# Two chained deformable-convolution blocks on one core: half-strip tap products on quarters of the array, and a new split between half-strips and gathered tiles

## The reference, cut to what matters

```python
x = x + relu(bn(deform_conv(_gn(x), offsets=conv3x3(_gn(x)))))        # L0, offsets below one pixel
v = _gn(x)
om1 = conv2d(v, w_om1, b_om1)                                         # 18 offsets + 9 masks per pixel
out = gelu(bn(modulated_deform_conv(v, offset1, sigmoid(m1), w_dcn1)))   # C1
om2 = conv2d(out, w_om2, b_om2)
out = modulated_deform_conv(out, offset2, sigmoid(m2), w_dcn2)        # C2
x = x + gelu(bn(out) + v)

# modulated_deform_conv: for each pixel and each of 9 taps, a bilinear sample at a data-dependent place
py = ys - PAD + ki + off[:, :, 0]; px = xs - PAD + kj + off[:, :, 1]
samp = bilinear_gather(x, py, px) * mask
out = einsum('bckhw,ock->bohw', samp, weight)
```

## Time and profile before

| | |
|---|---|
| median of the runs shown | 6692.59 us (6688.65 to 6696.53) |
| profiled execution, span | 6690.3 us |
| PE busy | 6000.0 us, 90% |
| DVE busy | 4534.0 us, 68% |
| ACT busy | 2208.6 us, 33% |
| POOL busy | 4608.7 us, 69% |
| indirect DMAs on POOL (L895) | 4752 = 132 tiles of 36, mean 967 ns |
| granted TensorE clock, mean | 0.928 |

### The profile page before, as it was taken

One profiled execution on the slowest core, in us unless ns is written; L12 is line 12 of the kernel. 1 busy time (PEld: TensorE's weight loads), 2 busy tenths in 40 slices (PEclk: granted clock), 3 DMA queues, 4 the chain that ended last, 5 costly groups with the idle time before them and its releaser, 6 DMA issues. The chain is left out here.

```text
span 6690.3 us, 124828 instructions
## 1 busy us (share of the span) xinstructions
PE 6000.0 (90%) x48293; PEld 4792.9 (72%) x48293; DVE 4534.0 (68%) x8624; ACT 2208.6 (33%) x3376; POOL 4608.7 (69%) x4765
## 2 busy tenths in 40 slices
PE   6997998987988988998987998899989989998996
PEld 6886777766777767777765666677767777776775
DVE  6886776856777856777754555477667767676675
ACT  1222222232222222222322222244434444443442
POOL 0005777766777767777777777777777777777776
PEclk9998999988999988999987898899989999998998
DMA  5334344435343433444422332333333334333333
GB/s 148 99 99 116 100 112 114 113 88 141 100 112 104 119 82 108 109 111 107 110 79 75 82 78 73 98 87 84 84 94 95 91 80 103 91 88 86 87 84 77
DMA packets 505472, 653.42 MB, mean 98 GB/s; under 512 B 116137, under 2 KB 412121, under 8 KB 496985
## 3 DMA queue, kind: packets, MB, share of 16 engines
q0 software_dynamic: 152064, 311.73, 18.8%
q1 hardware_dynamic: 352856, 333.94, 17.7%
HBM read 599.16 MB, written 46.15 MB: 96 GB/s over the span
## 5 line engine op out<-in xcount | busy, mean ns | idle before, releaser
L895 POOL DMA_INDIRECT G<-table,IDX x4752 | 4594.6, 967 | 2036.7 <-issue 1932.9
L2282 DVE TENSOR_TENSOR ARENA<-ARENA,OUT 128x864 f32<-128x864 f32 x936 | 937.5, 1048 | 142.7 <-PE RED L1123 94.7
L1517 ACT ACTIVATE SAMP<-RED 96x384 f32<-96x384 f32 x688 | 335.2, 487 | 1889.8 <-PE RED L1335 824.9
L1123 PE MATMUL RED<-IDENT,ARENA 128*96 128x128 f32 x7344 | 876.1, 279 | 73.0 <-DVE ARENA L2282 73.0
L2085 DVE TENSOR_TENSOR G<-G,WPS 128x1152 f32<-128x1152 f32 x528 | 711.1, 1347 | 309.3 <-DMA G<-table,IDX 308.0
L1123 PEld LDWEIGHTS RED<-IDENT,ARENA 128*96 128x96 f32 x7344 | 816.5, 129 | 117.4 <-issue 114.3
L1316 PE MATMUL BTP<-PAD,ARENA 80*128 x2304 | 748.5, 448 | 56.8 <-DVE ARENA L2078 29.9
L1072 PE MATMUL OFF<-PAD,ARENA 128*54 128x128 f32 (+1 forms) x10944 | 748.5, 295 | 12.7 <-ACT PAD L1417 6.8
L1072 PEld LDWEIGHTS OFF<-PAD,ARENA 128*54 128x54 f32 (+1 forms) x10944 | 666.9, 134 | 112.9 <-issue 97.5
L1196 PE MATMUL BTP<-X 80*128 80x480 f32 x1248 | 648.7, 638 | 105.8 <-ACT X L1461 57.0
L1512 ACT ACTIVATE SAMP<-RED 96x384 f32<-96x384 f32 x528 | 257.3, 487 | 1450.4 <-PE RED L1138 733.7
(11 more groups left out here) (216 smaller groups left out, 7777.7 us busy)
## 6 DMA issues: line engine op xcount, KB each, us to landing
ARENA<-wtab SPq DMA_DIRECT2D x416, 400.0 KB
G<-table,IDX POOLq DMA_INDIRECT x4752
ARENA<-xo SPq DMA_DIRECT2D x96, 720.0 KB
X<-xo SPq DMA_DIRECT2D x80, 360.0 KB, 3.8
table<-TB SPq DMA_DIRECT2D x64, 384.0 KB, 2.5
X<-x SPq DMA_DIRECT2D x3, 3200.0 KB, 18.2
out<-X SPq DMA_DIRECT2D x20, 320.0 KB
wtab<-TB SPq DMA_DIRECT2D x16, 384.0 KB, 3.1
```

Source lines behind the costliest of these rows:

```text
L895: pool.indirect_dma_start(G[:, b, k, :], None, tables[seg.table], bass.IndirectOffsetOnAxis(ap=IDX[:, q, b * TAPS + k:b * TAPS + k + 1], a ...
L1123: last = nc.tensor.matmul(RED[b % 2][0:TPG * C, gr * 128:(gr + 1) * 128], PROD[gr][:, sft, :], IDENT[:, :], start=(sft == 0), stop=(sft == ...
L1517: nc.scalar.activation(SAMP[:, x], RED[x][0:TPG * C, 0:GROUPS * 128].rearrange("p (g n) -> p g n", g=GROUPS), ACT.Copy).then_inc(z.samp_re ...
L2282: nc.vector.tensor_tensor(out=PROD[gr].rearrange("p (dy dx) (j c) -> p j dy dx c", dy=3, j=TPG), in0=win.rearrange("p j dy (dx c) -> p j d ...
```

## The change

Half-strips: the 80 columns are cut in two overlapping sides of 64 columns that lie on partitions 0 to 63 and 64 to 127 (`XW`, `XSTEP`). For one tap there are now four matmuls of 64x64 by 64x480, one for each side and image: side picks the array's rows and the PSUM bank, the image picks the array's columns. So one bank holds both images of one side, and both banks are filled by each tap; the next tap waits until both are read. The 18 products on DVE and the six groups of 15 transposing matmuls stay as many. The tents are made in two pieces, taps 0 to 4 and taps 5 to 8, on 128 partitions in place of 80. Samples of a half-strip go to `SAMP1` in three copies in place of two.

Split: pairs 0 to 2 use rows 32 to 64 for half-strips (16 of them) and have 17 gathered tiles. Kind x is not used any more: the mix is 26 d and 14 f, "ddf" * 8 + "df" and "ddf" * 4 + "df". Tail and pair 3 keep their steps. In a step with a successor of kind f, the first piece of the next tents stands on ACT ahead of the tile's last sample and the half-strip's last sample.

```diff
-MIXED_C = "xdxdfd" + "xdxfd" * 3, "xdxdfd" + "xdxdf"
+MIXED_C = "ddf" * 8 + "df", "ddf" * 4 + "df"
-C1_ROWS = {0: (32, 48), 1: (32, 48), 2: (32, 48), 3: (32, 64)}
+C1_ROWS = {0: (32, 64), 1: (32, 64), 2: (32, 64), 3: (32, 64)}
+XW, XSTEP = 64, W - 64
+TX_TAPS = (0, 5), (5, TAPS)
...
-                def taps_half(half, im, gr):
+                def taps_half(half, k):
...
-                        if c >= len(TAPS1[p]):
-                            pe.wait_ge(weighted1, c + 1 - len(TAPS1[p]))
-                        row = strip_row(seg, t // 2) + t % 2 * 2 + k // 3 - 1 - BELOW1 - r0
-                        nc.tensor.matmul(TAPS1[p][c % len(TAPS1[p])][:, 0:TAPW1], TX1[p][im][:, k, :],
-                                         XT1[p][:, im, row:row + WY1, :].rearrange("p w c -> p (w c)"),
-                                         start=True, stop=True).then_inc(taps1, 1)
+                    if h or k:
+                        pe.wait_ge(weighted1, 18 * h + 2 * k)
+                    row = strip_row(seg, t // 2) + t % 2 * 2 + k // 3 - 1 - BELOW1 - r0
+                    for side in range(2):
+                        ps_ = slice(XW * side, XW * side + XW)
+                        for im in range(2):
+                            last = nc.tensor.matmul(BTP[side][64 * im:64 * im + 64, 0:TAPW1], TX1[p][ps_, k, im, :],
+                                                    XT1[p][ps_, im, row:row + WY1, :].rearrange("p w c -> p (w c)"),
+                                                    start=True, stop=True)
+                        last.then_inc(taps1, 1)
...
+                def weight_half(half, k):
+                    for side in range(2):
+                        at = 2 * gr + side
+                        if j == 0:
+                            dve.wait_ge(prod_used, half.wg + GROUPS + max(0, at - 1))
+                        dve.wait_ge(taps1, 18 * half.i + 2 * k + side + 1)
...
                     if half.prep:
                         on.offsets(*half.prep)
-                    tile_sample(2)
+                    if step.ahead:
+                        on.tents1(*step.ahead, 0)
                     tile_sample(3)
-                    half_sample(1)
+                    half_sample(2)
                     if half.prep:
                         on.mask(*half.prep)
```

More of the change, by code:

```diff
@@ L1233, in consume_both @@
                         pe.wait_ge(e, column_evacs(half.seg.p, side))
-                    tiles = [(b, 0, step.po, b // 2) for b in range(UNITS)]
-                    halves = [(im, 1, half.po, 0) for im in range(2)]
-                    on.taps_half(half, 0, 0)
+                    on.taps_half(half, 0)
                     if step.prep:
                         on.convolve(*step.prep)
-                    on.taps_half(half, 0, 1)
-                    on.reduce_half(half, 0, 0)
+                    on.taps_half(half, 1)
@@ L1251, in consume_both @@
-                    on.reduce_half(half, 1, 0)
-                    on.project_units(step, [tiles[1], halves[0]], 5)
+                    on.reduce_half(half, 0, 0)
+                    on.taps_half(half, 3)
+                    on.reduce_half(half, 1, 0)
+                    on.project_tile(step, 0)
+                    on.taps_half(half, 4)
+                    on.turn_unit(step, 1)
+                    on.taps_half(half, 5)
+                    on.project_tile(step, 1)
+                    on.reduce_half(half, 0, 1)
@@ L1788, in constants1 @@
                         nc.vector.memset(to.iota[:, w:w + 1], float(w))
-                    nc.vector.memset(to.column[:, 128:256], 0.0)
-                    nc.vector.tensor_copy(to.below_row, BASE_Y[:, 0:1])
-                    for c in range(TC):
-                        nc.vector.tensor_scalar(to.steps[:, c:SCOLS:TC], BASE_X[96:98, 0:SCOLS // TC * TAPS:TAPS], float(c), None, ALU.add)
-                    last = nc.vector.scalar_tensor_tensor(out=to.negp, in0=BASE_Y[0:W, 0:1], scalar=-float(TC), in1=BASE_X[0:W, 0:1],
+                    nc.vector.memset(to.column[:, 128:182], 0.0)
@@ new lines, in constants1 @@
+                    half_cols, half_taps = SCOLS // 2, SCOLS // 2 // TC * TAPS
+                    for side in range(2):
+                        for c in range(TC):
+                            nc.vector.tensor_scalar(to.steps[:, side * half_cols + c:(side + 1) * half_cols:TC],
+                                                    BASE_X[96:98, side * half_taps:(side + 1) * half_taps:TAPS], float(c - XSTEP * side), None, ALU.add)
+                    last = nc.vector.tensor_scalar(to.below_row, BASE_Y[:, 0:1], float(XW // TC), -float(XW // TC), ALU.is_ge, ALU.mult)
@@ L1847, in prepare_half_strips @@
                     after(0)
+                    places = turned(seg, t)[:, :, :, 1:2 * TAPS:2]
+                    most, least = (m.rearrange("p (tt side k) -> p tt side k", tt=2, side=2) for m in (lent_.smax, lent_.sneg))
+                    nc.vector.scalar_tensor_tensor(out=most[:, :, 0], in0=places[:, :, 0], scalar=float(WY1 - XW), in1=most[:, :, 0],
+                                                   op0=ALU.add, op1=ALU.max)
+                    nc.vector.scalar_tensor_tensor(out=least[:, :, 1], in0=places[:, :, 1], scalar=-1.0, in1=least[:, :, 1],
+                                                   op0=ALU.mult, op1=ALU.max)
                     nc.vector.tensor_scalar(FLAT[:, :].rearrange("p (tt im k) -> p tt im k", tt=2, im=2), turned(seg, t)[:, :, :, 0:2 * TAPS:2],
```

255 lines of the change are left out of this document (144 added, 111 removed).

## The result

The changed kernel takes 7,035.97 us (median; 7,035.38 to 7,036.55) against 6,692.59: a ratio of 1.0517 with a 95% interval of 1.0492 to 1.0543. It is slower. The prediction was 7,073 with a range of 6,815 to 7,315 and a chance of 0.83 for slower.

A forecast was written before the change was run, and what follows sets the result against it. POOL was taken to run near its pace with PE right behind, so steps were priced on PE: 6690.3 us plus 359 for mixes and 21 for tails, 7,070, with 2.3 over the profiled span 7,073 us; range 6,815 to 7,315.

The forecast's parts named there:

- The mixes: Pairs 0 to 2: 26 d and 14 f steps make 949 us each, 359 us more in all than before.
- the tails: Ends of pairs 0 to 2: 7 us more per pair, 21 us more together.
- POOL's 540 us are a gain: Pairs 0 to 2: 12 gathered tiles fewer per pair shorten the kernel; chance 0.07, most of it within 2%.
- PE stands right behind POOL: Kernel before: POOL runs close to its pace throughout, with PE busy 715.8 of 786.4 us in pair 1's mix.
- A dense step of 16.6 us: Each d step in the mixes of pairs 0 to 2 stays at 16.6 us.
- Four quarters at once: Taps on PE: a tap's four products run together, 0.9 us per tap, 8.1 us for nine.
- two at a time: Rival for the taps: 1.7 us per tap, f steps of 38.5 and 47 us, 7,315 us in all; chance 0.12.
- An even f step: Mixes: 27.1 us of PE work plus 5.7 us of waits, 32.8 us against 35.6 before.
- An odd f step: Mixes: adds convolution and an end stall on DVE; next d starts at 39.7 us, 41.1 with the slower clock.
- The tents ahead of the samples: Last f of a mix: first tents wait on offsets through DRAM and delay the last samples, 7 us more per pair.
- The first f behind the norm: Tails of pairs 0 to 2: the one f with a gain there saves 2.8 us.
- Pair 3 and C2: 69 tiles at POOL's pace, about 46 us each; the two stages give and cost nothing.

The follow-up runs named there:

- The quarters alone: Changed kernel with the earlier split of tiles and half-strips put back, four quarter matmuls per tap kept: 6,650.07 us, ratio 0.9937 against the kernel before.

## Why the prediction was right, point by point

**The method held.** I priced steps on PE, not tiles on POOL. The forecast was +380 us and +343 was measured. The mixes came 7 us above their forecast of +359, the tails 50 us below theirs, and the head and the stages behind added 6 that had been put at nothing. Close as the total is, it is no proof of the tails' part, which had the wrong sign. The rival in which POOL's 540 us are a gain lost, and the experiment with fewer gathers shows why: the changed mixes don't react to POOL at all (912.3 and 912.4 us).

**"PE stands right behind POOL" failed.** I read POOL's even pace through the mix as the bound there. Before, PE's chain of steps set the mixes (786 us in pair 1) and POOL's floor was 10 us below. An engine that keeps its pace without a wait may still be served just in time. The sum didn't suffer, since it took the mixes' measured length.

**A dense step of 16.6 us: right**, 19, 18 and 16 of the 26 in the three mixes (two of pair 2's take 14.3, at the end of its last dense work). The ones behind an odd f take 18.5 to 19.3, 1.9 to 2.7 us more where I had put 1.4, and the first of a mix takes 17.9 to 18.5.

**Four quarters at once: right**, 0.97 us from a tap to the next work where I took 0.9. The rival "two at a time" would have been 1.7.

**An even f step: 32.0 us, 32.8 forecast, from two terms that were both off.** I put PE's work at 27.1 and the waits at 5.7. The trace has 2.9 us of idle entries: before taps 2, 5, 7 and 8, as walked, with 1.05, 0.61, 0.75 and 0.52 us for my 1.2, 0.8, 1.5 and 0.8. The wait before tap 4 and the one at the end aren't there. The rest, 29.1, is 2 us over my 27.1. The nine taps account for 0.6 of it. Part of the other 1.4 may be overlap that a stall takes away: a tile's group of six (L1138) gives way to the next group after 0.66 to 0.69 us in the even f step of the earlier trace rows, and in the rows above (L1157) after 0.86 or more where PE then has to wait or has only just waited. Four times 0.2 us would be 0.8 (an estimate from these rows); I didn't test it by itself. If so, an idle entry understates its stall.

**An odd f step: 39.1 us, 39.7 forecast**, with PE's wait of 4.17 us at its end where 4 to 5 were named. DVE's chain is the one that was walked: the mask is there after 34.4 us (34.6 forecast), the preparation takes 3.5 (3.7), and the first product's group starts 1.2 us later (1.0). The experiment that moves the preparation shows the stall to be that chain on DVE.

**A mix: 955, 956 and 951 us from its first group to its last, 949 (957 for pair 0) forecast.** The split can be checked the same way from PE's side alone. It takes 12 tiles out of x steps at 11.1 us, 133 (8 of them go into f steps), and adds 8 f steps whose mean is 36.6 (32.0, and 39.2 + 2 for the d behind), 293: +160. Measured between the stretches that POOL doesn't hold: 912.3 - 762.7 = 150.

**The tails: -29 us, +21 forecast: wrong.** Three terms. The tents ahead of the samples were to cost 7 us per pair. The wait of that size is there (6.6 to 7.2 us), but the last f of a mix is only 0.4 to 1.4 us longer than before: the f behind the norm waited 11.5 to 12.8 us for it before and now waits 7.5 to 7.8. The run with the tents late puts the order's cost in that step at 2.6 to 3.2 us. A delay in front of a step that waits anyway is mostly absorbed; the prediction had walked the delay and not the wait behind it. The first f behind the norm was to save 2.8 us and saves 7.7 to 8.7 (53.8, 54.7 and 54.1 us before; 46.1, 46.0 and 45.5 now). The quarters alone do the same (45.4, 45.9 and 45.1 us), down to POOL's 45 for a tile. The rest of the tail, with its turned columns, was to cost 3 us more and lies between 4.6 less and 1.0 more.

**Pair 3 and C2: right.** 3,191.6 us from their first gather to the end, 46.3 for each of the 69 tiles, and 3,188.8 before. The quarters' shorter steps are lost there, since POOL sets the pace of both: PE's busy time in about 693 us of pair 3 is 541 us, where it was 624.

**POOL in the mixes.** 621 us of busy and issue in pair 0's mix, where 620 to 650 were forecast. But the waits of a tile were 20 and 30 us in turn, with a few others between 13 and 36, not 15 to 20: 330.8 us in the first 911.7 us of that mix.

## What to carry to other kernels

Trade work between engines by the price that each unit has on the engine that will be last after the change: here 11 us of PE for a gathered tile against some 25 (an f step's mean of 36.6 less the tile in it) for a half-strip that replaces half a tile. That the other engine is full says nothing yet; leave out a slice of its work and see whether the stage moves. When two engines are level to within a per cent or so, an edit that speeds up the slower one alone gives only that much, and the other one's pace then sets the time.

## What the runs showed of the hardware that I had not expected

- A stall's second half. A wait of 4.17 us on PE was followed by 5 us at a mean granted clock of 0.60, between the levels of 1.2 and 2.4 GHz, and cost 2 us more in the next step. A wait of 2.73 us was followed by 5 us at 0.50 and cost 2.8; the same wait in another run by 5 us at 0.71, and cost 1.4. With the wait at 1.15 us the clock was 1.00 in the 5 us behind it. 3 us of stall removed were worth 5.
- Four 64x64 fp32 products of 480 columns span 1.03 us, two 64x128 ones 1.07 us, one 80x128 1.07 us. Going between the quarters and full-width work 9 times a step costs little, about 0.1 us each at most by this comparison: a tap's slot is 0.97 to 1.00 us where a product in one of the groups of three of before takes 0.90 to 0.97. The Trainium skill's page "TensorEngine Tiling (Array Packing)", section Tiling Modes, says that a change of tiling mode drains the engine. No row here shows a drain by itself; if there is one, it hides in that.
- The order of the quarters, rows or columns first, moved an f step by no more than 0.2 us. By the rule in the Trainium skill's "TensorE: Matmul & The Clock Gate", Part 3, that weight loads overlap running matmuls only on other row groups, one of the two should have been slower. Neither run shows that effect.
- With the quarters and the old split, POOL issued 616 indirect DMAs in 776.0 us with next to no waits on other engines (0.9 us between 1,700 and 2,300 us): 1.26 us each, of which some 0.95 are the instruction. In C2 the busy and issue time of the kernel before is 1.27 us per DMA (1,815.7 + 563.7 us, 1,872 DMAs), so the pace is about the same in both stages.
